# Two-bank context attention, early first weights of an eight-expert stage, and sixteen experts' weights kept in a 32-expert stage

## The chip, the cores and the metric

The kernel runs on one core of one Trainium2 chip. It is one launch that holds a whole four-layer decoder. The metric is the device time of one execution in microseconds, less is better; the time before is the median of three runs.

## The reference

The input x has 8 sequences of 256 tokens with 256 features; a context of 120 tokens with 192 features belongs to each sequence. Twelve sublayers follow each other, each as x = layernorm(x + f(x)). All is float32. The three that the change touches are these:

```
# L0 ffn: 8 experts, the best one for each token
e = argmax(softmax(x @ gate_w));  out = p[e] * (gelu(x @ w1[e] + b1[e]) @ w2[e] + b2[e])
# L1 ffn: 32 experts, the best four, at most 256 tokens for each, and one shared expert
probs, idx = top_k(softmax(x @ gate_w.T), 4);  weights = probs / sum(probs)
out = sum_k weights[k] * ((silu(g) * u) @ w_down[idx[k]]),  g, u = split(x @ w_gate_up[idx[k]])
out += (silu(gs) * us) @ shared_w_down
# L3 xattn: 8 heads of 64, keys and values from the context
out = softmax(q @ k.T * 64**-0.5) @ v,  then out @ Wo + bo
```

## The kernel before, in words

Activations are kept transposed in SBUF as xT, 128 partitions by 2 halves by 2048 tokens. The stages run one after the other. Each is made of blocks; in a block every engine has its own instruction list, engines are ordered by semaphores alone (`wait_ge`, `then_inc`), and a block begins when all engines have ended the one before. Each stage ends with a layer norm. SP issues plain DMAs, POOL (GpSimd) the indirect ones, each in program order; nothing is planned automatically.

**L3x, the context attention of layer 3** (`attention_stage`, the branch from L688). There are 16 units u, a sequence and half of the heads each. For a unit TensorE computes the scores (L725) into banks 0 and 1, VectorE takes their maxima (L828), TensorE turns these (L735) into bank 7, ScalarE copies them negated (L792), TensorE computes the turned scores less the maxima (L748, L753) into banks 2 and 3, ScalarE takes the exponential (L809) into PT, and TensorE forms the value products in bank 4 (L765) and the sums of the exponentials in bank 6 (L768). ScalarE inverts the sums as exp(-ln(sum)) (L799 and L801); VectorE (`divide`) corrects this inverse by one Newton step in two instructions (L837, L838) and multiplies the value products by it (L839). TensorE's order in the loop is: turned scores of u, values of u-1, maxima of u+1, scores of u+2. The values of a unit wait for its exponential and for `at_done` of the unit before (L761), as bank 4 and bank 6 are used by every unit. VectorE's order is maxima of u, then division of u-2.

**L0f, the eight-expert stage** (`moe_top1_stage`). The first block routes: TensorE and VectorE compute each token's expert and its slot in the array slots_x in HBM (`slot`) and, for each tile of 256 slots, which expert's weights it needs (`weight_row`, then `routed`). POOL then scatters the rows of each of 16 token tiles into slots_x (L1455); ahead of each scatter but the first it waits until all before have landed (L1454, semaphore `put`). Behind the scatters it issues two indirect gathers of the weights of tiles 0 and 1 (L1424, 2.1 MB each) and waits for `put`. In the same block TensorE and VectorE go on with the bias term and the sum (L1495, L1561). The second block works through 15 tiles: SP loads the slots (L1589), TensorE transposes (L1627), multiplies up (L1639) and down (L1652); POOL gathers weights two tiles ahead.

**L1f, the 32-expert stage** (`moe_top4_stage`). Block one routes on TensorE and VectorE (L2467 to L2532) while SP prefetches only the next stage's packed weights. Block two: TensorE transposes x, ScalarE copies it into rows (L2591), POOL scatters each tile four times into picks_x (L2549, 64 scatters), and the shared expert is computed beside that. Block three loops over 32 experts. SP loads for expert e its weights into `we` (L2634, four slots) and its picked rows into `xe` (L2635, four slots), both counted on one semaphore; the loads for e+4 are issued when ScalarE has finished expert e (`y_done`). TensorE's order is transposes of e+2 (L2667), up of e+1 (L2677), down of e (L2687). ScalarE does the silu (L2706) and the scaled copy out (L2714), VectorE the copy of the transposes (L2729), the product (L2754) and the places of the results (`place`). POOL scatters the results in two DMAs per expert into picks_y (L2652), and ScalarE writes ye of e+2 only when those of e have landed. A fourth block reads picks_y back and sums.

Of the kernel before, what the change touches and what calls it, by code (L numbers as in the profile page):

```python
# [18 lines left out]
P = 128  # L19
# [34 lines left out]
def columns(*fields):  # L54
    at, out = 0, {}
    for name, n in fields:
# [46 lines left out]
           "y_ready", "mean_ready", "d_ready", "sq_ready", "var_ready", "x_ready", "veps_ready", "ln_ready",  # L103
# [5 lines left out]
           "got_head2", "got_head3", "zeroed", "filled", "ticked", "routed", "centred", "used", "dotted", "placed", "blanked", "sent_even", "sent_odd", *(f"tile{t}" for t in range(16)),  # L109
# [143 lines left out]
def attention_stage(nc, c, name):  # L253
# [55 lines left out]
    with ExitStack() as ctx:  # L309
# [378 lines left out]
        else:  # L688
# [3 lines left out]
            with ExitStack() as part:  # L692
# [4 lines left out]
                cor = sb("cor", [P, 2 * SEQ], F32, part)  # L697
# [10 lines left out]
                with nc.Block() as block:  # L708
# [5 lines left out]
                    def _(pe):  # L714
# [103 lines left out]
                    def _(dve):  # L818
# [12 lines left out]
                        def divide(u):  # L831

                            b, half = units[u]
                            guess = inv[:, u % 2, :]
# [562 lines left out]
def moe_top1_stage(nc, c, ins):  # L1397
# [16 lines left out]
    with ExitStack() as ctx:  # L1414
# [14 lines left out]
        with ExitStack() as part:  # L1429
# [10 lines left out]
            with nc.Block() as block:  # L1440
# [5 lines left out]
                def _(pool):  # L1446

                    pool.wait_ge(s["filled"].sem, FILLS[0] * 16)
                    pool.wait_ge(s["routed"].sem, s["routed"].at(1))
                    for t in range(NT):  # L1450
                        pool.wait_ge(s["row_ready"].sem, s["row_ready"].at(t + 1))
                        if t:

                            pool.wait_ge(s["put"].sem, s["put"].at(16 * t))  # L1454
# [3 lines left out]
                    gather_weights(0)  # L1458
# [967 lines left out]
def moe_top4_stage(nc, c, ins):  # L2426
# [9 lines left out]
    SLOTS = E * CAP  # L2436
    with ExitStack() as ctx:
# [5 lines left out]


        with ExitStack() as part:
# [168 lines left out]
        with ExitStack() as part:  # L2614
            NB = 4
            we = sb("we", [P, NB, 2 * 2 * I + D], F32, part)
# [11 lines left out]
            with nc.Block() as block:  # L2628
                @block.sync
                def _(sp):  # L2630
                    def load(e):

                        k = e % NB
                        sp.dma_start(we[:, k, :], ins["L1f_w"][e]).then_inc(s[x_in[k]].sem, 16)  # L2634
                        sp.dma_start(xe[:, k, :, :], c.picks_x[e * CAP:(e + 1) * CAP, :]  # L2635
                                     .rearrange("(q p) d -> p q d", p=P)).then_inc(s[x_in[k]].sem, 16)
                    for e in range(NB):
                        load(e)
                    for e in range(E):
# [19 lines left out]
                def _(pe):  # L2659
                    def turn(e):  # L2660

                        pe.wait_ge(s[x_in[e % NB]].sem, s[x_in[e % NB]].at(32 * (e // NB + 1)))
# [8 lines left out]
                    def up(e):  # L2671
                        pe.wait_ge(s["evac_a"].sem, s["evac_a"].at(e + 1))
                        if e >= 2:
                            pe.wait_ge(s["hidden"].sem, s["hidden"].at(e - 1))
                        for g in range(2):
                            for j in range(DH):
                                mm = nc.tensor.matmul(ps[:, 2 + e % 2, g * CAP:(g + 1) * CAP],  # L2677
                                                      we[:, e % NB, j * 2 * I + g * I:j * 2 * I + g * I + I],
# [3 lines left out]
                    def down(e):  # L2682
# [3 lines left out]
                        for q in range(2):  # L2686
                            mm = nc.tensor.matmul(ps[:, 4 + e % 2, q * D:(q + 1) * D], a[:, e % 2, q * P:(q + 1) * P],  # L2687
                                                  we[:, e % NB, 4 * I:4 * I + D], start=True, stop=True)
                        mm.then_inc(s["down_pe"].sem, 1)
                    turn(0)  # L2690
# [33 lines left out]
                def _(dve):  # L2724
# [8 lines left out]
                    def place(e):  # L2733

                        k = e % NB
                        dve.wait_ge(s[x_in[k]].sem, s[x_in[k]].at(32 * (e // NB + 1)))
# [688 lines left out]
```

## Time and profile before

| | us |
|---|---|
| median of 3 runs | 3403.5 (3394.33 to 3407.84) |
| profiled execution | 3397.96 |
| its span, first to last instruction | 3396.1 |
| TensorE matmuls busy | 2415.3 |
| VectorE busy | 1693.9 |
| ScalarE busy | 937.2 |
| GpSimd busy | 787.2 |

Busy times overlap, and their sum says nothing of the span. The mean granted TensorE clock is 0.855 of full speed; the clock has two levels in this trace. Line numbers (L765) are those of the kernel. Times in a timeline are microseconds from the span's start: L0f lies from about 335 on, L1f from 1190, L3x's attention loop from 3056 to 3167. An entry in brackets is the idle time of the engine ahead of the instruction and what ended it.

### The profile page before, as it was taken

Reading aid. Unit: us, or ns where it says so; the run is one execution under the profiler, and the core shown is the slowest. Engines: PE = TensorE matmul, PEld = TensorE weight load, DVE = VectorE, ACT = ScalarE, POOL = GpSimd, SP = SyncE. Lnnn points to the kernel's source line nnn. Section 1 sums busy time; section 2 is a strip of 40 time slices with the busy share of each in tenths; the row PEclk is TensorE's granted clock in tenths of the full one; section 3 lists DMA queues with packets and bytes.
Section 4 is the critical chain, followed back from the end, with each engine's and each line's share of the span. In section 5 each row is a group of like instructions: output and inputs, shape, how many; then the busy total and the mean of one; then the engine's idle time right before and its main releaser. Section 6 shows DMA issues by size and latency. Waiting matters only on the chain. (4 is left out here: it accounts for less than half of the span.)

```text
span 3396.1 us, 38901 instructions
## 1 busy us (share of the span) xinstructions
PE 2415.3 (71%) x13893; PEld 1562.2 (46%) x13899; DVE 1693.9 (50%) x4532; ACT 937.2 (28%) x1761; POOL 787.2 (23%) x772
## 2 busy tenths in 40 slices
PE   6777489798776652758763565777777776488786
PEld 4534278645434332633441222666666654236332
DVE  4644100148446631353746567556656636534387
ACT  0232022110430410221141232433333323223244
POOL 1000200230010034411000001777777760100000
PEclk9889599899997966977996578899899887799898
DMA  6200145334015114635001002422222210000000
GB/s 168 65 14 17 63 147 186 121 93 126 20 42 143 26 62 143 221 145 99 4 23 62 0 0 83 103 54 58 54 56 57 63 38 25 0 25 1 0 0 25
DMA packets 125964, 223.41 MB, mean 66 GB/s; under 512 B 38550, under 2 KB 76182, under 8 KB 122208
## 3 DMA queue, kind: packets, MB, share of 16 engines
q1 hardware_dynamic: 72688, 116.33, 12.1%
q0 software_dynamic: 51952, 100.65, 9.7%
q10 hardware_dynamic: 1152, 4.19, 0.3%
q8 instruction: 101, 1.65, 0.2%
q14 instruction: 71, 0.58, 0.1%
HBM read 240.93 MB, written 62.59 MB: 89 GB/s over the span
## 5 line engine op out<-in xcount | busy, mean ns | idle before, releaser
L2897 POOL DMA_INDIRECT L2f_G<-in_L2f_table,L2f_idx x512 | 523.1, 1022 | 232.0 <-issue 155.8
L2954 PE MATMUL psum<-L2f_G,L2f_diag 128*128 128x256 f32 x1024 | 299.8, 458 | 172.7 <-ACT L2f_diag L3024 172.7
L2954 PEld LDWEIGHTS psum<-L2f_G,L2f_diag 128*128 128x128 f32 x1024 | 232.9, 233 | 237.2 <-ACT L2f_diag L3024 196.0
L3132 DVE CUSTOM_DVE_ANT_0 L2f_junk<-L2f_G,L2f_X 128x256 bf16<-128x256 f32 x512 | 182.7, 421 | 257.0 <-DMA L2f_G<-in_L2f_table,L2f_idx 257.0
L3024 ACT ACTIVATE L2f_diag<-const,L2f_actd 128x128 f32<-128x128 f32 x528 | 161.2, 388 | 25.2 <-DVE L2f_actd L3146 25.0
L1156 PE MATMUL psum<-constb 128*128 128x256 bf16 x512 | 83.9, 290 | 82.0 <-ACT L2a_PT L1323 24.3
L2931 PE MATMUL psum<-xT,L2f_mw 128*128 128x256 f32 x512 | 122.5, 383 | 0.0
L2549 POOL DMA_INDIRECT picks_x<-L1f_rows,L1f_put x64 | 61.5, 960 | 246.1 <-ACT L1f_rows L2591 227.3
L1639 PE MATMUL psum<-L0f_xeT,L0f_we 128*128 128x256 f32 x480 | 108.7, 386 | 0.9 <-DVE L0f_xeT L1674 0.9
L1652 PE MATMUL psum<-L0f_we,L0f_h 128*128 128x256 f32 x480 | 106.1, 380 | 0.0
L1323 ACT ACTIVATE L1a_PT<-psum 128x1536 f32<-128x1536 f32 x32 | 46.4, 1450 | 207.3 <-PE psum L1291 207.3
L2931 PEld LDWEIGHTS psum<-xT,L2f_mw 128*128 128x128 f32 x512 | 97.3, 193 | 12.9 <-issue 0.2
L1156 PEld LDWEIGHTS psum<-constb 128*128 128x128 bf16 x512 | 41.8, 101 | 129.5 <-ACT L1a_PT L1323 32.9
L3017 ACT ACTIVATE L2f_actd<-L2f_dots 128x9 f32<-128x9 f32 (+1 forms) x64 | 13.5, 211 | 317.2 <-DVE L2f_dots L3132 317.2
L991 PE MATMUL psum<-xT,weights 128*128 128x512 f32 x192 | 89.5, 630 | 16.0 <-PEq L236 11.0
L1639 PEld LDWEIGHTS psum<-L0f_xeT,L0f_we 128*128 128x128 f32 x480 | 93.2, 194 | 14.1 <-issue 1.3
L1652 PEld LDWEIGHTS psum<-L0f_we,L0f_h 128*128 128x128 f32 x480 | 90.3, 191 | 11.4
L1666 ACT ACTIVATE L0f_h<-psum,L0f_we 128x256 f32<-128x256 f32 x120 | 50.3, 470 | 155.3 <-PE psum L1639 155.3
L2652 POOL DMA_INDIRECT picks_y<-L1f_ye,L1f_home x64 | 61.3, 958 | 93.7 <-ACT L1f_ye L2714 83.0
L2196 POOL PARTITION_ALL_REDUCE L2x_gm<-L2x_mx x4 | 1.4, 357 | 349.2 <-issue 325.8
L2667 PE MATMUL psum<-const,L1f_xe 128*128 128x128 f32 x128 | 22.5, 303 | 82.9 <-DMA L1f_xe<-picks_x 82.5
L1674 DVE COPY L0f_xeT<-psum 128x512 f32<-128x512 f32 x15 | 10.4, 692 | 138.4 <-PE psum L1627 138.4
(670 smaller groups left out, 5162.9 us busy)
## 6 DMA issues: line engine op xcount, KB each, us to landing
L1f_we<-in_L1f_w SPq DMA_DIRECT2D x32, 384.0 KB, 3.1
picks_x<-zeros SPq DMA_DIRECT2D x16, 544.0 KB, 8.9
L1f_xe<-picks_x SPq DMA_DIRECT2D x32, 272.0 KB, 3.7
picks_y<-zeros SPq DMA_DIRECT2D x16, 512.0 KB, 7.0
L2f_G<-in_L2f_table,L2f_idx POOLq DMA_INDIRECT x512, 2.8
slots_x<-zeros POOLq DMA_DIRECT2D x8, 512.0 KB, 7.5
L1f_g<-picks_y SPq DMA_DIRECT2D x8, 512.0 KB, 10.9
L1f_g<-picks_y ACTq DMA_DIRECT2D x8, 512.0 KB, 12.0
```

The lines of the kernel that those rows point to most:

```text
L991: mm = nc.tensor.matmul(dst, wt[rows, j * m + g * P:j * m + g * P + P], source[rows, j, bass.ds(col, n)], start=(k == 0), stop=(k == len(t ...
L1156: nc.tensor.matmul(out, c.one, m.broadcast_to([P, 2, P]), start=True, stop=False, skip_group_check=True)
L1639: mm = nc.tensor.matmul(ps[:, f // 2, (f % 2) * TILE:(f % 2 + 1) * TILE], we[:, k, j * F + f * P:j * F + f * P + P], xeT[:, k, j, :], star ...
L1652: mm = nc.tensor.matmul(ps[:, 6 + k, q * D:(q + 1) * D], h[:, k, f, q * P:(q + 1) * P], we[:, k, W2 + f * D:W2 + (f + 1) * D], start=(f == ...
L1666: nc.scalar.activation(h[:, k, f, :], ps[:, f // 2, (f % 2) * TILE:(f % 2 + 1) * TILE], ACT.Gelu, bias=we[:, k, B1 + f:B1 + f + 1]).then_i ...
L2549: nc.gpsimd.indirect_dma_start(out=c.picks_x[:, :], out_offset=bass.IndirectOffsetOnAxis(ap=put[:, t, k:k + 1], axis=0), in_=rows[:, t, :] ...
L2652: nc.gpsimd.indirect_dma_start(out=c.picks_y[:, :], out_offset=bass.IndirectOffsetOnAxis(ap=home[:, e % NB, q:q + 1], axis=0), in_=ye[:, e ...
L2897: nc.gpsimd.indirect_dma_start(out=G[:, h, k, :], out_offset=None, in_=ins["L2f_table"], in_offset=bass.IndirectOffsetOnAxis(ap=IDX[:, t, ...
L2931: mm = nc.tensor.matmul(ps[:, UP_BANK + i % 2, chunk(g)], wt[:, j * F + f * P:j * F + f * P + P], c.xT[:, j, chunk(k)], start=(j == 0), st ...
L2954: mm = nc.tensor.matmul(ps[:, MIX_BANK + t % 2, 0:D], diag[:, i % 2, k, :], row[:, D:2 * D], start=(h == 0 and k == 0), stop=(h == HEADS - ...
L3024: e = nc.scalar.activation(diag[:, i % 2, k, :], c.ident, ACT.Copy, scale=act_d[:, i % 2, k:k + 1])
L3132: e = V.tensor_tensor_reduce(out=junk[:, k, :], in0=row[:, 0:D], in1=X[:, t % 3, :], scale=1.0, scalar=0.0, op0=ALU.mult, op1=ALU.add, acc ...
```

## The change

In L3x the value products go to bank 4 or 5 in turn. They wait for the logarithm of the unit before (which has read bank 6) and for the division of the unit before that. The Newton step is left out: the division is one multiplication by exp(-ln(sum)). In L0f the gather of the first tile's weights is issued ahead of the scatters, and a scatter no longer waits for the ones before. In L1f a buffer of 16 experts' weights lives from the routing to the end of the expert loop. SP issues the first 16 loads in the routing block; TensorE waits for all of them at the head of the expert loop. In the loop SP loads only xe for e+4 when expert e is done and, behind it, the weights of e+16 into the slot that e has left. The semaphore counts follow.

```diff
@@ L3x, TensorE values(u)
-                                pe.wait_ge(s["at_done"].sem, s["at_done"].at(u))
+                                pe.wait_ge(s["ln_ready"].sem, s["ln_ready"].at(u))
+                            if u >= 2:
+                                pe.wait_ge(s["at_done"].sem, s["at_done"].at(u - 1))
-                                nc.tensor.matmul(ps[rows_of(i), 4, j * SEQ:(j + 1) * SEQ], V[0:CTX, b, h * hd:(h + 1) * hd],
+                                nc.tensor.matmul(ps[rows_of(i), 4 + u % 2, j * SEQ:(j + 1) * SEQ], V[0:CTX, b, h * hd:(h + 1) * hd],
@@ L3x, VectorE divide(u)
-                            link(nc.vector.tensor_tensor(cor[:, :], ps[:, 6, :], guess, ALU.mult))
-                            link(nc.vector.scalar_tensor_tensor(cor[:, :], cor[:, :], -2.0, guess, ALU.add, ALU.mult))
-                            nc.vector.scalar_tensor_tensor(AT[:, 2 * half:2 * half + 2, b * SEQ:(b + 1) * SEQ],
-                                                           ps[:, 4, :].rearrange("p (g q) -> p g q", g=2), -1.0,
-                                                           cor[:, :].rearrange("p (g q) -> p g q", g=2), ALU.mult, ALU.mult)\
+                            nc.vector.tensor_tensor(AT[:, 2 * half:2 * half + 2, b * SEQ:(b + 1) * SEQ],
+                                                    ps[:, 4 + u % 2, :].rearrange("p (g q) -> p g q", g=2),
+                                                    inv[:, u % 2, :].rearrange("p (g q) -> p g q", g=2), ALU.mult)\
                                 .then_inc(s["at_done"].sem, 1)
@@ L0f, POOL in the routing block
+                    gather_weights(0)
                     for t in range(NT):
                         pool.wait_ge(s["row_ready"].sem, s["row_ready"].at(t + 1))
-                        if t:
-                            pool.wait_ge(s["put"].sem, s["put"].at(16 * t))
                         nc.gpsimd.indirect_dma_start(
...
-                    gather_weights(0)
                     gather_weights(1)
@@ L1f, SP in the routing block
                     c.prefetch(sp, name)
+                    for e in range(NW):
+                        sp.dma_start(we[:, e, :], ins["L1f_w"][e]).then_inc(s["w_first"].sem, 16)
@@ L1f, SP in the expert loop
-                        sp.dma_start(we[:, k, :], ins["L1f_w"][e]).then_inc(s[x_in[k]].sem, 16)
                         sp.dma_start(xe[:, k, :, :], c.picks_x[e * CAP:(e + 1) * CAP, :]
                                      .rearrange("(q p) d -> p q d", p=P)).then_inc(s[x_in[k]].sem, 16)
+                    def load_weights(e):
+                        if e >= NW + 2:
+                            sp.wait_ge(s[w_in[e % 2]].sem, s[w_in[e % 2]].at(16 * ((e - NW) // 2)))
+                        sp.dma_start(we[:, e % NW, :], ins["L1f_w"][e]).then_inc(s[w_in[e % 2]].sem, 16)
...
                         if e + NB < E:
                             load(e + NB)
+                        if e + NW < E:
+                            load_weights(e + NW)
@@ L1f, TensorE
                     def up(e):
                         pe.wait_ge(s["evac_a"].sem, s["evac_a"].at(e + 1))
+                        if e >= NW:
+                            pe.wait_ge(s[w_in[e % 2]].sem, s[w_in[e % 2]].at(16 * ((e - NW) // 2 + 1)))
...
+                    pe.wait_ge(s["w_first"].sem, s["w_first"].at(16 * NW))
                     turn(0)
```

NW is 16 (experts' weights held), NB is 4 (slots of xe), CAP is 256.

## Rows read from the trace of the kernel before

**Rows 1.** The page's first part: busy us, share of the span, instructions of each engine.
```profile
PE 2415.3 (71%) x13893; PEld 1562.2 (46%) x13899; DVE 1693.9 (50%) x4532; ACT 937.2 (28%) x1761; POOL 787.2 (23%) x772
```

**Rows 2.** Timeline, one L3x unit: start us, us, engine, line, what, idle before.
```profile
3096.80 0.69 DVE L837 TENSOR_TENSOR L3x_cor<-psum,L3x_inv 128x512 f32<-128x512 f32 x1 [3.00 <-ACT L3x_inv L801]
...
3097.42 0.60 PE L753 MATMUL psum<-L3x_MT,const 64*120 64x256 f32 x4
...
3098.26 0.69 DVE L839 SCALAR_TENSOR_TENSOR L3x_AT<-psum,L3x_cor 128x512 f32<-128x512 f32 x1
...
3099.09 1.08 PE L765 MATMUL psum<-L3x_PT,L3x_V 120*64 120x256 f32 x8 [1.08 <-ACT L3x_PT L809]
...
3101.72 0.59 ACT L799 ACTIVATE L3x_inv<-psum 128x512 f32<-128x512 f32 x1
...
3102.33 0.60 PE L748 MATMUL psum<-L3x_Q,L3x_K 64*120 64x256 f32 x4
...
3105.30 1.09 PE L765 MATMUL psum<-L3x_PT,L3x_V 120*64 120x256 f32 x8 [1.07 <-ACT L3x_PT L809]
```

**Rows 3.** Waits, 3055 to 3170: total us, times, longest.
```profile
PE psum L765 <- ACT L3x_PT L809: 14.0, 13, 1.1
...
PE psum L765 <- DVE L3x_AT L839: 5.0, 2, 3.6
```

**Rows 4.** Timeline, last L3x unit.
```profile
3160.60 1.98 PE L765 MATMUL psum<-L3x_PT,L3x_V 120*64 120x256 f32 x8 [3.61 <-DVE L3x_AT L839]
```

**Rows 5.** Timeline, L0f from the first scatter to the first tile load.
```profile
365.64 1.08 POOL L1455 DMA_INDIRECT slots_x<-L0f_rows,L0f_slot  x1 [73.86 <-DVE L0f_weight_row L1552]
...
390.23 1.22 DVE L1561 TENSOR_TENSOR L0f_acc<-psum,xT 128x1024 f32<-128x1024 f32 x1 [3.87 <-PE psum L1495]
...
413.75 0.96 POOL L1455 DMA_INDIRECT slots_x<-L0f_rows,L0f_slot  x1 [2.22 <-DMA slots_x<-L0f_rows,L0f_slot]
...
416.31 0.96 POOL L1424 DMA_INDIRECT L0f_we<-in_L0f_w,L0f_weight_row  x1 [0.30 <-DMA slots_x<-L0f_rows,L0f_slot]
429.80 4.45 SPq L1589 DMA_DIRECT2D L0f_xe<-slots_x  x3
```

**Rows 6.** The tile L0f_we: landing of the 15 weight gathers.
```profile
DMA to landing us min/median/max: 8.8/9.2/12.5
```

**Rows 7.** Timeline, L1f: last scatter, first loads, first up projection.
```profile
1314.04 0.96 POOL L2549 DMA_INDIRECT picks_x<-L1f_rows,L1f_put  x1 [0.30 <-issue]
1322.16 0.36 SPq L2634 DMA_DIRECT2D L1f_we<-in_L1f_w  x1
...
1330.16 3.62 PE L2677 MATMUL psum<-L1f_xeT,L1f_we 128*128 128x256 f32 x8
```

**Rows 8.** Timeline, L1f expert loop: first and last reload, and two experts between.
```profile
1337.89 0.33 SPq L2634 DMA_DIRECT2D L1f_we<-in_L1f_w  x1
...
1354.33 0.33 SPq L2634 DMA_DIRECT2D L1f_we<-in_L1f_w  x1
...
1354.70 0.44 SPq L2635 DMA_DIRECT2D L1f_xe<-picks_x  x1
...
1358.86 0.66 PE L2667 MATMUL psum<-const,L1f_xe 128*128 128x128 f32 x4 [1.49 <-DMA L1f_xe<-picks_x]
...
1363.01 0.33 SPq L2634 DMA_DIRECT2D L1f_we<-in_L1f_w  x1
...
1453.74 0.33 SPq L2634 DMA_DIRECT2D L1f_we<-in_L1f_w  x1
```

**Rows 9.** DMA issues of L1f and L0f: KB each, median us to landing.
```profile
L1f_xe<-picks_x SPq DMA_DIRECT2D x32, 272.0 KB, 3.7
...
L0f_xe<-slots_x SPq DMA_DIRECT2D x3, 256.0 KB, 2.7
```

**Rows 10.** Windows: length, busy by engine, PE clock, DMA share, GB/s; routing, return loads.
```profile
1190.00:1232.00 42.00, 14.43 (x65) 13.79 (x66) 24.43 (x100) 0.63 (x1) 0.00 (x0) 0.50 0.07 26
...
1477.00:1505.00 28.00, 11.03 (x32) 4.62 (x32) 22.07 (x48) 0.00 (x0) 0.00 (x0) 0.50 0.76 301
```

More of the change, by code:

```diff
@@ L102 @@
            "negmax", "probs", "turned", "evac_a", "evac_b", "mixed", "normed", "at_ready", "at_evac", "out_ready",
-           "y_ready", "mean_ready", "d_ready", "sq_ready", "var_ready", "x_ready", "veps_ready", "ln_ready",
+           "y_ready", "mean_ready", "d_ready", "sq_ready", "var_ready", "x_ready", "ln_ready",
            "root_ready", "exp_ready", "newton", "dve_chain", "loaded", "pack_even_landed", "pack_odd_landed", "route_pe", "route_dve",
@@ L108 @@
            "x_even", "x_odd", "y_even", "y_odd", "y_done", "got_even", "got_odd", "got_head0", "got_head1",
-           "got_head2", "got_head3", "zeroed", "filled", "ticked", "routed", "centred", "used", "dotted", "placed", "blanked", "sent_even", "sent_odd", *(f"tile{t}" for t in range(16)),
+           "got_head2", "got_head3", "zeroed", "filled", "ticked", "routed", "used", "placed", "blanked", "sent_even", "sent_odd", "w_first", "w_even", "w_odd", *(f"tile{t}" for t in range(16)),
            *(f"expert{k}" for k in range(4)),
@@ L696, in attention_stage @@
                 inv = sb("inv", [P, 2, 2 * SEQ], F32, part)
-                cor = sb("cor", [P, 2 * SEQ], F32, part)
                 ones = sb("ones", [P, P], F32, part)
@@ L2436, in moe_top4_stage @@
     SLOTS = E * CAP
+    NB, NW = 4, 16
+    WE = 2 * 2 * I + D
+    w_in = ("w_even", "w_odd")
     with ExitStack() as ctx:
@@ L2442, in moe_top4_stage @@
         acc = sb("acc", [P, DH, T])
+        early = ctx.enter_context(ExitStack())
+        we = sb("we", [P, NW, WE], F32, early)
         with ExitStack() as part:
@@ L2614, in moe_top4_stage @@
         with ExitStack() as part:
-            NB = 4
-            we = sb("we", [P, NB, 2 * 2 * I + D], F32, part)
             xe = sb("xe", [P, NB, 2, ROW], F32, part)
@@ L2660, in turn @@
                     def turn(e):
-                        pe.wait_ge(s[x_in[e % NB]].sem, s[x_in[e % NB]].at(32 * (e // NB + 1)))
+                        pe.wait_ge(s[x_in[e % NB]].sem, s[x_in[e % NB]].at(16 * (e // NB + 1)))
                         if e >= 2:
@@ L2677, in up @@
                                 mm = nc.tensor.matmul(ps[:, 2 + e % 2, g * CAP:(g + 1) * CAP],
-                                                      we[:, e % NB, j * 2 * I + g * I:j * 2 * I + g * I + I],
+                                                      we[:, e % NW, j * 2 * I + g * I:j * 2 * I + g * I + I],
                                                       xeT[:, e % 2, j, :], start=(j == 0), stop=(j == DH - 1))
@@ L2687, in down @@
                             mm = nc.tensor.matmul(ps[:, 4 + e % 2, q * D:(q + 1) * D], a[:, e % 2, q * P:(q + 1) * P],
-                                                  we[:, e % NB, 4 * I:4 * I + D], start=True, stop=True)
+                                                  we[:, e % NW, 4 * I:4 * I + D], start=True, stop=True)
                         mm.then_inc(s["down_pe"].sem, 1)
+                    pe.wait_ge(s["w_first"].sem, s["w_first"].at(16 * NW))
                     turn(0)
@@ L2735, in place @@
                         k = e % NB
-                        dve.wait_ge(s[x_in[k]].sem, s[x_in[k]].at(32 * (e // NB + 1)))
+                        dve.wait_ge(s[x_in[k]].sem, s[x_in[k]].at(16 * (e // NB + 1)))
                         if e >= NB:
@@ L2761, in moe_top4_stage @@
             for k, n in dict(turned=E, evac_a=E, hidden_pe=E, hidden=E, down_pe=E, gated=E, y_done=E,
-                             expert0=16 * E // 2, expert1=16 * E // 2, expert2=16 * E // 2, expert3=16 * E // 2, sent_even=16 * E, sent_odd=16 * E, placed=E).items():
+                             expert0=4 * E, expert1=4 * E, expert2=4 * E, expert3=4 * E,
+                             w_first=16 * NW, w_even=8 * (E - NW), w_odd=8 * (E - NW), sent_even=16 * E, sent_odd=16 * E, placed=E).items():
                 s[k].base += n
+        early.close()
         with ExitStack() as part:
```

1 line of the change is left out of this document (removed).

## The prediction

> **What bounds the kernel now.** I read the page's busy shares first: TensorE has 71% of the span [rows 1], so no engine is a wall, and the twelve stages have limits of their own. I therefore read each of the three stages that the diff touches by its timeline, and then its waits and DMA landings. In the attention loop of the last context stage (L3x) one unit takes 6.21 us. The reader is to see in it that TensorE ends the turned scores at 3098.02, stands still for 1.08 us, and starts the value products only when VectorE's third instruction has freed the bank at 3098.95 [rows 2]. The trace names the exponential L809 as releaser, but the one that the products need was over a unit earlier, and the products' loads begin before this one ends. So I read the 13 such waits as waits for `at_done` [rows 3]. In the eight-expert stage (L0f) the routing ends with 16 scatters that run one by one, 3.2 us apart, while the last VectorE work is over at 391.45; the tile loop's first load is issued at 429.80 [rows 5]. In the 32-expert stage (L1f) TensorE waits in the expert loop for the picked rows (xe), not for weights: two experts take 8.68 us from issue to issue, of which 4.16 lie between the issue of xe and the first transpose [rows 8].
>
> **Attention, two banks and one division.** Removed: two VectorE instructions of 0.69 us in each of 16 units. Moved: the value products of unit u now need the division of u-2 and the logarithm of u-1 instead of the division of u-1. Added wait: the logarithm (`ln_ready`). Everything later on TensorE queues behind it. It ends at 3102.31 [rows 2], one unit ahead of the products at 3105.3, which could start at the earliest at 3104.2, so it is hidden by 1.9 us. If this cover went, the unit would lengthen by what is missing. What is late next is TensorE itself: 6.21 - 1.08 = 5.13 us per unit. VectorE has less to do than before, ScalarE the same. The maxima copy keeps its distance, since it hangs on TensorE's own order. Sum: 13 units x 1.08 = 14.0. The two last ones waited 5.0 in total [rows 3]: of unit 14's 1.42 I take 1.1; unit 15 waited 3.61 [rows 4] and will wait for one logarithm only, about 0.8, so 2.8. The final division loses two instructions: 1.4. Unit 15's first eight products took 1.98 at the lower clock after that idle time, against 1.08 in a usual unit [rows 2, 4]; with both sets, 1.7. Together 21.0. Bounds: 15 (the logarithm's wait costs half of each stall again, or the clock still falls) and 25 (the output projection behind it also starts at the full clock).
>
> **Eight-expert stage.** The first gather of weights moves ahead of the scatters: 1.26 us in POOL's queue. Each scatter no longer waits until the one before has landed. The nearest row for a scatter behind a scatter is L1f's: 0.96 busy and 0.30 idle, 1.26 us apart [rows 7]. From 365.64: gather, 16 scatters, second gather issued at 365.64 + 17 x 1.26 = 387.1 instead of 416.31, so 29.2 earlier. Beside them TensorE and VectorE do their bias products until 391.45 as before. What is late next is the second gather's landing, since 13.49 us pass from its issue to SP's next DMA [rows 5], far more than the block's change on other engines needs. Two gathers in flight land after up to 12.5, a single one in 9.2 [rows 6]. With the first long landed I take off half of the 3.3 us between these: gain 31. Bounds: 22 (the 2.1 MB of the first gather stand ahead of the scatters in the same queue and hold them for a whole 9.2 us), 34 (it ends with VectorE). If the scatters' speed needed VectorE's silence it would be lost here, since four adds now run beside them.
> [...]
>
> **32-expert stage.** Sixteen more DMAs on SP's queue during routing, behind the next pack's load: 16 x 0.36 us of issue [rows 7] = 6 us, and 6.3 MB, 21 us at the 301 GB/s of this stage's own return loads [rows 10]. Routing lasts 42 us and the DMA engines carried 26 GB/s in it [rows 10], so both are hidden, and the wait `w_first` at the head of TensorE's queue costs nothing. If the cover were gone (loads slower than 150 GB/s), all experts would start later. Below nothing I bound it by -3: something else that must come by DMA in these 42 us meets the loads and lands 1 us later, as xe does behind one of them [rows 9], three times. I take 0. The 64 scatters between routing and experts stay: POOL paces them.
> Start of the loop: before, four pairs of loads were issued from 1322.16 and the first up projection began at 1330.16 [rows 7]. Now only xe is loaded: 1322.16 + 2.7 to 3.7 for landing, then two sets of transposes, 0.66 each at the full clock [rows 8] and twice that at the low one, beside the second of which the first is copied: about 1328. Gain 2.2.
> In the loop: y_done(e), SP issues xe(e+4), landing, transpose, up, down, two copies, y_done(e+2). From 1358.86 to 1363.01 that tail is 4.15 [rows 8]; with 0.37 for the weights' issue ahead and 4.16 for xe it makes 8.68. The 0.37 goes for certain. xe lands in 3.7 with 384 KB ahead of it in the same queue; the nearest load without such a forerunner, 256 KB for L0f, lands in 2.7 [rows 9]. The return scatters stay, so I take 2.9. Per expert: (0.37 + 0.8) / 2 = 0.585; 28 loads, 16.4. Mean pace 4.29 (27 intervals from 1337.89 to 1453.74 [rows 8]) becomes 3.7. The weights for expert e+16 are issued behind xe(e+4), so that they delay only a load that comes 3.7 us later; TensorE waits for them sixteen experts later, which costs nothing, and SP's new waits for earlier weight loads neither. What is late next: the same chain, then TensorE's own work of some 3 us per expert, and the return scatters. Bounds: 0.37/2 x 28 = 5, and (0.37 + 1.0)/2 x 28 = 19 plus some low-clock stretches saved. Sum for the stage 19.
>
> **The sum.** 21 + 31 + 19 = 71. The profiled execution took 3397.96 (span 3396.10, 1.86 around it); less 71 is 3327. It stood 5.5 below the median of the three runs (3403.5) and 3 below the mean of all four, 3401. I forecast from this mean: 3330.
>
> **Rivals.**
> (a) The picked rows land no sooner: the early weights are off the path. For it: what TensorE waits for is xe, never weights [rows 8], and 272 KB in 256 short rows may need its 3.7 by itself. Against: L0f's 2.7 [rows 9]. Then only SP's 0.37 counts, 5 instead of 16.4: 3341. The same figure holds if the return scatters take over at 3.9 per expert. Chance 0.22.
> (b) The L0f scatters don't overlap, because the gather blocks them or each is served alone: pace 3.2 stays. L1f's 64 scatters speak against it. The stage then gains 2 (one gather in flight at the end): 3359. Chance 0.05.
> (c) The clock holds. Where TensorE stands still for 3.61 us, its next products run at the 1.2 GHz level [rows 4]. With shorter waits in both loops and a shorter gap ahead of the output projection, stretches at 1.2 GHz go too. A burst there costs nearly its own length again (1.98 against 1.08 [rows 2, 4]); 9 us of it less in three places: 3321. The Trainium skill has this as a rule: "TensorE: Matmul & The Clock Gate", section "HAM oscillation", idle gaps between bursts throttle the clock anew. Chance 0.12.
> (d) Slower. Both loops get denser on TensorE, and the granted clock falls to 1.2 GHz for their length. L3x: 16 units x 5.1 = +82; L1f: 28 experts x 3.0 = +84; 3496. It decides once the low level holds for more than two fifths of both loops. Against: units at 83% busy run at the full level now [rows 2]. Chance 0.03, with all else that could lose 71 us.
> My own case, all three paid as worked out, has 0.58: 3330, between 3319 and 3343.
>
> **How the numbers follow.** About 0.5% (17 us) is what a measurement of this kernel can tell from no change. (a) and (c) lie within 3312 to 3352, which also takes in the lower ends of two terms at once, not of all three (22 + 15 + 5: 3359). Faster by over 0.5%: 0.96; within: 0.01; slower: 0.03.
>
> **What would show it.** L3x: units 5.1 us apart, no idle time ahead of the value products but in the last, one VectorE instruction of 0.69 per division. L0f: POOL's DMAs 1.26 us apart, SP's first tile load 29 to 34 us sooner after routing. L1f: sixteen 384 KB loads over before routing ends, xe landing in 2.9, the loop's issues 3.7 apart. The prediction is wrong if the scatters stay 3 us apart, if xe still needs 3.7, or if TensorE waits for the logarithm.

## The result, and the profile after

| | before | after |
|---|---|---|
| median, us | 3401.3 (4 runs) | 3325.1 (4 runs, 3316.55 to 3328.6) |
| profiled execution | 3397.96 | 3316.55 |
| its span | 3396.1 | 3314.7 |

The ratio is 0.9775, 95% interval 0.9754 to 0.9796: the changed kernel is 76 us faster (69 to 84), where 3330 was forecast, 71 us. Its profiled execution is the shortest of its four, so the terms are compared by stage. The page's first part, beside [rows 1]:

```profile
PE 2402.9 (72%) x13893; PEld 1553.9 (47%) x13899; DVE 1672.6 (50%) x4500; ACT 937.5 (28%) x1761; POOL 787.6 (24%) x772
```

VectorE has 32 instructions less, two for each of 16 units. Its busy time fell by 21.3 us, that of TensorE's matmuls by 12.4, the others' by less. So most of the time saved is time in which TensorE had stood still.

**L3x.** Timeline of one unit, which answers to [rows 2], and of the last one:

```profile
3029.19 0.69 DVE L836 TENSOR_TENSOR L3x_AT<-psum,L3x_inv 128x512 f32<-128x512 f32 x1 [3.30 <-ACT L3x_inv L802]
...
3030.33 1.08 PE L766 MATMUL psum<-L3x_PT,L3x_V 120*64 120x256 f32 x8
...
3035.39 0.87 PE L766 MATMUL psum<-L3x_PT,L3x_V 120*64 120x256 f32 x6
...
3083.36 1.08 PE L766 MATMUL psum<-L3x_PT,L3x_V 120*64 120x256 f32 x8 [0.74 <-issue]
...
3086.63 0.69 DVE L836 TENSOR_TENSOR L3x_AT<-psum,L3x_inv 128x512 f32<-128x512 f32 x1 [1.99 <-ACT L3x_inv L802]
...
3087.65 9.66 PE L863 MATMUL psum<-L3x_AT,weights 128*128 128x512 f32 x18 [2.34 <-PEq L707]
```

The products start 5.06 us apart (3030.33 and 3035.39) with no bracket, so without idle time. One division of 0.69 us is left. The last products wait 0.74 us instead of 3.61 and run at the full clock, 1.08 against 1.98 [rows 4]. The output projection of the kernel before:

```profile
3167.78 12.66 PE L866 MATMUL psum<-L3x_AT,weights 128*128 128x512 f32 x22 [3.80 <-PEq L708]
```

From the first scores to the output projection the stage takes 89.6 us (2998.08 to 3087.65) instead of 111.7 (3056.05 to 3167.78): 22.2 less. The output projection's first result reaches VectorE 8.84 us after its start instead of 10.13: 1.3 more.

**L0f.** The last routing instruction before, and behind it the timeline after, from that instruction to the first tile load, which answers to [rows 5]:

```profile
364.58 0.17 DVE L1552 CAST L0f_weight_row<-L0f_owner 128x15 uint32<-128x15 f32 x1
```

```profile
360.68 0.17 DVE L1546 CAST L0f_weight_row<-L0f_owner 128x15 uint32<-128x15 f32 x1
...
361.76 1.09 POOL L1421 DMA_INDIRECT L0f_we<-in_L0f_w,L0f_weight_row  x1 [74.22 <-DVE L0f_weight_row L1546]
...
369.62 0.97 POOL L1450 DMA_INDIRECT slots_x<-L0f_rows,L0f_slot  x1 [0.30 <-issue]
369.73 1.22 DVE L1555 TENSOR_TENSOR L0f_acc<-psum,xT 128x1024 f32<-128x1024 f32 x1 [8.08 <-PE psum L1489]
370.89 0.97 POOL L1450 DMA_INDIRECT slots_x<-L0f_rows,L0f_slot  x1 [0.30 <-issue]
...
383.63 0.98 POOL L1421 DMA_INDIRECT L0f_we<-in_L0f_w,L0f_weight_row  x1 [0.30 <-issue]
385.01 1.23 DVE L1555 TENSOR_TENSOR L0f_acc<-psum,xT 128x1024 f32<-128x1024 f32 x1 [3.87 <-PE psum L1489]
393.47 4.50 SPq L1583 DMA_DIRECT2D L0f_xe<-slots_x  x3
```

POOL's DMAs stand 1.27 us apart, also the one that began while VectorE was in its first add. From the last routing instruction (it starts at 360.68, before at 364.58) to the first tile load it is 32.8 us instead of 65.2: 32.4 less. The block now ends long after VectorE (386.24); 9.84 us pass from the second gather's issue to SP's load, 13.49 before. The scatters are issued at their own pace, but the first eight land later than before, 2.6 to 7.8 us after their issue beside the first gather's 2.1 MB, where a scatter alone took 2.4.

**L1f.** Timeline: the early loads in the routing, the head of the loop, two experts, and the first load that reads the results back:

```profile
1153.35 8.34 SPq L2460 DMA_DIRECT2D L1f_we<-in_L1f_w  x16
...
1285.27 1.92 SPq L2632 DMA_DIRECT2D L1f_xe<-picks_x  x4
...
1290.03 2.50 PE L2683 MATMUL psum<-L1f_xeT,L1f_we 128*128 128x256 f32 x5
...
1300.72 0.36 SPq L2632 DMA_DIRECT2D L1f_xe<-picks_x  x1
...
1301.13 0.51 SPq L2638 DMA_DIRECT2D L1f_we<-in_L1f_w  x1
...
1304.61 0.36 SPq L2632 DMA_DIRECT2D L1f_xe<-picks_x  x1
1304.79 0.66 PE L2671 MATMUL psum<-const,L1f_xe 128*128 128x128 f32 x4 [1.08 <-DMA L1f_xe<-picks_x]
...
1418.78 1.28 SPq L2781 DMA_DIRECT2D L1f_g<-picks_y  x3
```

The same load before:

```profile
1477.14 2.87 SPq L2772 DMA_DIRECT2D L1f_g<-picks_y  x4
```

The DMA issues of the loop, median landing last, beside [rows 9]:

```profile
L1f_xe<-picks_x SPq DMA_DIRECT2D x32, 272.0 KB, 2.9
...
picks_y<-L1f_ye,L1f_home POOLq DMA_INDIRECT x64, 2.6
```

Windows of the routing and of two parts of the loop (columns as in [rows 10]):

```profile
1153.00:1195.00 42.00, 14.44 (x65) 13.81 (x66) 24.44 (x100) 0.63 (x1) 0.00 (x0) 0.50 0.45 175
1304.00:1344.00 40.00, 33.85 (x171) 27.84 (x172) 18.47 (x65) 12.80 (x32) 19.97 (x21) 1.00 0.77 244
1357.00:1397.00 40.00, 35.26 (x180) 29.15 (x179) 19.27 (x69) 13.44 (x33) 21.10 (x22) 1.00 0.47 150
```

The early loads put 175 GB/s on the routing's idle DMA engines, and from the next pack's load to the loop's first it takes 132.3 us, before 132.2: they cost nothing. The first up projection begins 4.76 us behind the first load instead of 8.00 [rows 7]. The picked rows land in 2.9 us instead of 3.7. From the first load of the loop to the first one that reads the results back it takes 133.5 us (1285.27 to 1418.78) instead of 155.0 (1322.16 to 1477.14): 21.5 less. The pace is 3.73 us per expert between 1304.61 and 1353.06, where weights are still loaded, and 3.63 afterwards (11 intervals from 1356.56 to 1396.49).

Not all of the 21.5 us is the queue's. In the loop before, TensorE fell twice to the lower clock level, and the changed loop has no such stretch:

```profile
1405.34 0.82 PE L2667 MATMUL psum<-const,L1f_xe 128*128 128x128 f32 x4 [2.05 <-DMA L1f_xe<-picks_x]
1405.95 3.46 PE L2677 MATMUL psum<-L1f_xeT,L1f_we 128*128 128x256 f32 x8
...
1439.99 1.11 PE L2667 MATMUL psum<-const,L1f_xe 128*128 128x128 f32 x4 [2.28 <-DMA L1f_xe<-picks_x]
1440.89 3.05 PE L2677 MATMUL psum<-L1f_xeT,L1f_we 128*128 128x256 f32 x8
```

Transposes and up projection of one expert take 4.28 and 4.16 us there, and 2.55 (0.66 + 1.89) at the full level: 3.3 us in all. All seven traces with this loop as it was (before, e1 to e6) have such stretches; between 4 and 21 of the 256 up-projection matmuls are slow in them, beside those of the loop's head. The traces of the changed kernel, of its repeat e9 and of e7 have none. The seven loops last 152.6 to 157.1 us, so a few us between two traces of L1f can be the execution's own.

22.2 + 32.4 + 21.5 + 1.3 = 77 us. These two executions differ by 81.4; the other 4 lie ahead of L0f, in stages that the change leaves alone (the last routing instruction starts at 360.68 instead of 364.58). The medians differ by 76.

### The profile page after: what moved, and what is told of

It reads as the page before. It is cut to its first block and busy times, and to the rows that moved or that the text cites. A ratio compares the mean times of both kernels' runs of the same rounds, so it can differ in the third digit from the quotient of the medians.

```text
span 3314.7 us, 38855 instructions
## 1 busy us (share of the span) xinstructions
PE 2402.9 (72%) x13893; PEld 1553.9 (47%) x13899; DVE 1672.6 (50%) x4500; ACT 937.5 (28%) x1761; POOL 787.6 (24%) x772
## 3 DMA queue, kind: packets, MB, share of 16 engines
q1 hardware_dynamic: 72688, 116.33, 12.4%
## 5 line engine op out<-in xcount | busy, mean ns | idle before, releaser
L1788 PE MATMUL psum<-L3f_h,weights 128*128 128x512 f32 x128 | 62.1, 630 | 22.1 <-DVE L3f_h L1859 22.0
L1421 POOL DMA_INDIRECT L0f_we<-in_L0f_w,L0f_weight_row x15 | 14.2, 948 | 264.9 <-PE psum L1646 190.4
## 6 DMA issues: line engine op xcount, KB each, us to landing
L1f_g<-picks_y SPq DMA_DIRECT2D x8, 512.0 KB, 12.3
L1f_g<-picks_y ACTq DMA_DIRECT2D x8, 512.0 KB, 12.3
```

The lines of the kernel that those rows point to most:

```text
L1788: mm = nc.tensor.matmul(ps[:, 4 + 2 * (n % 2) + o, :], w["w2"][:, f * D + o * P:f * D + o * P + P], h[:, u % 2, i * CH:(i + 1) * CH], star ...
```

## The experiments

The stages run one after the other, so each experiment is read by its stage in the trace, and by the ratio of the whole where that is wide enough. The first four ran on a chip on which the kernel before takes 3514.7 us (the untouched stage L2f alone takes 838.6 instead of 736.1 us there), the others on chips where it takes 3398 to 3399; ratios are always within one chip.

### e1, attention part alone


> The kernel before with the attention part of the change alone (two banks and one division). Theory: the three parts lie in stages that run one after the other and add up, so this one gives what the changed kernel's L3x shows: units 5.06 us apart, L3x shorter by 22 us, ratio 0.9935. Rival: part of the 22 us belongs to the run and not to the change, or to the other two parts (a shifted clock): then L3x is shorter by under 18 us.


Measured: ratio 0.9919 (0.9881 to 0.9958); units 5.06 us apart; first scores to output projection 3156.4 to 3246.0, 89.6 us as in the changed kernel. On the same chip e4, which leaves this stage alone, has 111.8. The 22 us belong to this part, and it does not lean on the others.

### e2, one division, one bank
```diff
-                            link(nc.vector.tensor_tensor(cor[:, :], ps[:, 6, :], guess, ALU.mult))
-                            link(nc.vector.scalar_tensor_tensor(cor[:, :], cor[:, :], -2.0, guess, ...))
+                            nc.vector.tensor_tensor(AT[...], ps[:, 4, :]..., inv[:, u % 2, :]..., ALU.mult)
                             # values(u) still waits for at_done.at(u), still bank 4
```


> The kernel before with the Newton step left out, but the value products still in one bank and still behind the division of the unit before. Theory: what binds before is one cycle, sums end, logarithm, exponential, three VectorE instructions, value products of the next unit, 6.21 us long. Without two instructions of 0.69 it is 4.83, under TensorE's own 5.06, so the second bank buys nothing: units 5.06 apart, no wait ahead of the value products but in the last units, L3x shorter by 20 to 22 us. Rival: the second bank is what frees TensorE: the wait for the division stays, and the unit falls by half of the stall or less, L3x shorter by under 12 us.


Measured: ratio 0.9947 (0.9918 to 0.9975). Its timeline, one unit:

```profile
3210.48 0.69 DVE L834 TENSOR_TENSOR L3x_AT<-psum,L3x_inv 128x512 f32<-128x512 f32 x1 [3.30 <-ACT L3x_inv L800]
...
3211.62 1.08 PE L764 MATMUL psum<-L3x_PT,L3x_V 120*64 120x256 f32 x8
...
3216.68 1.08 PE L764 MATMUL psum<-L3x_PT,L3x_V 120*64 120x256 f32 x8
```

The division ends at 3211.17, 0.45 us before TensorE is ready for the products at 3211.62, and the unit takes 5.06 us with one bank. The stage takes 92.5 us (3164.2 to 3256.7), 19.2 less than before, a little under the 20 to 22 of the first theory. Its mechanism holds: inside the loop the second bank buys nothing. The 2.9 us that two banks add lie at the end, where no other work stands ahead of the last products: they wait 2.2 us for the division there (0.74 in the changed kernel), and they and the sums behind them then run partly at the lower clock level, 1.73 and 1.98 us against 1.08 and 1.06. What the Newton step was there for is a better inverse; no run here measures what leaving it out costs in accuracy.

### e3, two banks, Newton step kept
```diff
-                            if u:
-                                pe.wait_ge(s["at_done"].sem, s["at_done"].at(u))
+                            if u >= 2:
+                                pe.wait_ge(s["at_done"].sem, s["at_done"].at(u - 1))
                             ...  # products into bank 4 + u % 2
+                            if u:
+                                pe.wait_ge(s["at_done"].sem, s["at_done"].at(u))
                             ...  # sums of the exponentials, bank 6
```


> The kernel before with the value products in bank 4 or 5 in turn, but the Newton step kept: since it reads bank 6, only the sums of the exponentials still wait for the division of the unit before. Theory (one cycle through the division): only the four value products, half of 1.08, move out of the cycle, 6.21 becomes 5.67, L3x shorter by 13 x 0.54 = 7 us, at most 9. Rival (the second bank is what frees TensorE): units 5.1 apart, L3x shorter by 14 us or more.


Measured: ratio 0.9962 (0.994 to 0.9984); the stage 96.6 us (3187.0 to 3283.6), 15.1 less. Its timeline, one unit:

```profile
3219.96 1.08 PE L765 MATMUL psum<-L3x_PT,L3x_V 120*64 120x256 f32 x8
...
3220.27 0.69 DVE L841 SCALAR_TENSOR_TENSOR L3x_AT<-psum,L3x_cor 128x512 f32<-128x512 f32 x1
...
3221.01 0.63 PEld L770 LDWEIGHTS psum<-L3x_PT,L3x_ones 120*64 120x64 f32 x8 [0.42 <-DVE L3x_AT L841]
...
3225.26 1.08 PE L765 MATMUL psum<-L3x_PT,L3x_V 120*64 120x256 f32 x8
```

The size in my expectation was wrong: 1.08 us are the value products alone, the sums take as much again, so 1.08 and not 0.54 moved out of the cycle. The 15.1 us are what the rival had forecast (14 or more), and the whole time alone would speak for it; what speaks against it is the trace. The cycle is still there: the sums wait 0.42 us for the division and the unit takes 5.31 us, where the rival had 5.1 and no wait. Either edit alone brings most of the 22 us; the division is the better half (19.2), and it needs no bank.

### e4, eight-expert part alone


> The kernel before with the eight-expert part alone (first gather ahead of the scatters, no wait between scatters). Theory: parts add up; from the last routing instruction to the first tile load 33 us instead of 65, ratio 0.9905. Rival: the gain of the stage hangs on what lies before it in the changed kernel (the run's own 3.8 us ahead of this stage): 28 us or less here.


Measured: ratio 0.9914 (0.9886 to 0.9942), 32.7 us from the last routing instruction to the first tile load (364.7 to 397.5), as in the changed kernel. So this part and that of L3x each bring alone what they bring in the changed kernel. The L1f part was not run alone as it stands.

### e5, no waits between the scatters, both gathers behind them


> The eight-expert part with the scatters' waits gone, but both gathers of weights behind the scatters as before. Theory: the waits were the cost (16 x 1.9 us), the place of the first gather is worth little: second gather issued at the same time as in the changed kernel (17 DMAs 1.27 us apart), but two gathers in flight at the end, so the first tile load comes 2 to 4 us later than in the changed kernel; the stage gains 29 us. Rival: with the 2.1 MB of the first gather no longer ahead of them the scatters land sooner and the block ends sooner: gain 33 or more.


Measured: ratio 0.9903 (0.9874 to 0.9932); 357.3 to 393.4, 36.1 us, 29.1 less than before. Its timeline:

```profile
378.75 1.00 POOL L1424 DMA_INDIRECT L0f_we<-in_L0f_w,L0f_weight_row  x1 [0.30 <-issue]
380.05 0.96 POOL L1424 DMA_INDIRECT L0f_we<-in_L0f_w,L0f_weight_row  x1 [0.30 <-DMA slots_x<-L0f_rows,L0f_slot]
...
393.41 0.89 SPq L1586 DMA_DIRECT2D L0f_xe<-slots_x  x2
```

13.36 us from the second gather to SP's load, as before (13.49); with the first gather long landed it is 9.84. So the waits are worth 29 us and the early first gather 3.3.

### e6, both gathers ahead of the scatters
```diff
                     gather_weights(0)
+                    gather_weights(1)
                     for t in range(NT):
                         ...
-                    gather_weights(1)
```


> The eight-expert part with both gathers ahead of the scatters. Theory: in the changed kernel the block ends with the landing of the second gather, 9.8 us behind its issue, since no other engine works then. With both ahead it ends with VectorE's last sum or the last scatter's landing: first tile load 6 to 7 us sooner than in the changed kernel, the stage gains 38 to 39 us. Rival: what ends the block is POOL's drain of its queue or the scatters' landing behind 4.2 MB: the first tile load comes at most 2 us sooner, gain 34 or less.


Measured: ratio 0.9868 (0.9838 to 0.9898); 362.5 to 389.8, 27.3 us, 37.9 less than before. Its timeline:

```profile
385.43 0.97 POOL L1454 DMA_INDIRECT slots_x<-L0f_rows,L0f_slot  x1 [0.30 <-issue]
388.12 1.22 DVE L1558 TENSOR_TENSOR L0f_acc<-psum,xT 128x1024 f32<-128x1024 f32 x1 [3.87 <-PE psum L1492]
389.79 0.89 SPq L1586 DMA_DIRECT2D L0f_xe<-slots_x  x2
```

SP's load follows VectorE's last add (which ends at 389.34) by 0.45 us. So what ended the block in the changed kernel was the second gather in flight: POOL waits there for nothing but the scatters, and still the next block did not begin until the gather had landed. The landings say the same: the second gather landed 12.5 us behind its issue before, 12.3 in e5, 8.8 in the changed kernel, and SP's load came 1.0 to 1.1 us behind the landing in all three. This is 5.5 us better than the changed kernel (6 to 7 were expected), and VectorE is now the end.

### e7, rows ahead of the weights, nothing else
```diff
-                        sp.dma_start(we[:, k, :], ins["L1f_w"][e]).then_inc(s[x_in[k]].sem, 16)
                         sp.dma_start(xe[:, k, :, :], ...).then_inc(s[x_in[k]].sem, 16)
+                        sp.dma_start(we[:, k, :], ins["L1f_w"][e]).then_inc(s[w_in[k]].sem, 16)
@@ up(e)
+                        pe.wait_ge(s[w_in[e % NB]].sem, s[w_in[e % NB]].at(16 * (e // NB + 1)))
```


> The kernel before with one edit in the 32-expert loop: for each expert SP issues the picked rows ahead of its weights, each on a semaphore of its own; transposes wait for the rows alone, the up projection for the weights. No early weights, no 16 slots. Theory A (what the change bought is that the rows no longer stand behind 384 KB; that the weights come early is not needed): loop 12 to 17 us shorter, issues 3.7 to 3.9 apart. Theory B (the traffic of 384 KB per expert itself slows the rows, wherever it stands in the queue, and the weights now arrive late for the up projection): loop at most 6 us shorter, TensorE waits for the weights. In the changed kernel the rows land in 3.0 us (3.6 at those with weights beside them) where weights are still loaded and in 2.7 where they are not, which speaks for A in the larger part.


Measured: ratio 0.9958 (0.9943 to 0.9973); loop 136.9 us (1324.7 to 1461.6), 18.1 less than before, of the changed kernel's 21.5. Its timeline:

```profile
1344.32 0.36 SPq L2635 DMA_DIRECT2D L1f_xe<-picks_x  x1
1344.53 0.66 PE L2668 MATMUL psum<-const,L1f_xe 128*128 128x128 f32 x4 [1.11 <-DMA L1f_xe<-picks_x]
1344.73 0.47 SPq L2637 DMA_DIRECT2D L1f_we<-in_L1f_w  x1
1345.02 1.89 PE L2679 MATMUL psum<-L1f_xeT,L1f_we 128*128 128x256 f32 x8
```

The up projection stands right behind the transposes, without a bracket: the weights, though loaded only four experts ahead and behind the rows, are there. The rows land in 3.0 us. Theory A holds, though 18.1 is more than its 12 to 17: this loop has none of the low-clock stretches, which are worth 3.3 us in the trace of the kernel before. 16 experts' weights in SBUF and their load during routing account for 3.4 us (1.4 against the repeat e9), which is within the 4.5 us by which unchanged loops differ. What can be placed of it is an up projection 0.9 us earlier at the head of the loop (5.7 us behind the first load here, 4.8 there), and an end, in which no weights are loaded, that is 1.4 us shorter (from the last load of rows to the first that reads back: 23.7 us here, 22.3 there).

### e8, eight slots for the picked rows
```diff
-    NB, NW = 4, 16
+    NB, NW = 8, 16
```


> The kernel before with the 32-expert part of the change, and eight slots for the picked rows instead of four (rows of expert e+8 are loaded when e is done). Theory: the loop is still bound by the chain from the end of expert e over the load of the rows of e+4 to its transposes, 3.7 us per expert while weights are loaded and 3.35 afterwards. With eight slots this chain leaves the path; next is TensorE's own work of some 3.0 us or the return scatters (1.27 x 2 and landing, every second expert's buffer): pace 3.0 to 3.2, loop shorter than in the changed kernel (133.5 us) by 8 to 16 us, though eight loads at the start cost up to 1 us. Rival: the second chain, the results' buffer behind its scatters' landing, has the same length as the first: pace stays at 3.4 or more and the loop is at most 5 us shorter.


L3x and L0f are as in the kernel before. Measured: ratio 0.9937 (0.9912 to 0.9961); loop 125.1 us (1325.3 to 1450.4), 8.4 less than in the changed kernel, at the lower end of what the theory said. Waits of the loop (total us, times, longest):

```profile
ACT L1f_ye L2727 <- DMA picks_y<-L1f_ye,L1f_home: 55.3, 25, 6.9
...
PE psum L2677 <- DMA L1f_xe<-picks_x: 52.9, 1, 52.9
```

TensorE's transposes no longer wait for rows but once, ahead of the loop. In their place ScalarE waits for the return scatters, 25 times where it was once before (1.9 us). A timeline of this kernel shows how:

```profile
1387.60 0.85 ACT L2727 ACTIVATE L1f_ye<-psum,L1f_own 128x256 f32<-128x256 f32 x2
...
1389.47 0.96 POOL L2662 DMA_INDIRECT picks_y<-L1f_ye,L1f_home  x1 [0.30 <-issue]
...
1395.67 0.84 ACT L2727 ACTIVATE L1f_ye<-psum,L1f_own 128x256 f32<-128x256 f32 x2 [6.94 <-DMA picks_y<-L1f_ye,L1f_home]
```

Two experts' results come out together (1386.61 and 1387.60) and their four scatters are issued 1.27 us apart. The results of the second next expert need the same buffer and wait until its two scatters have landed. Here, in the longest such wait, the second of them was issued at 1389.47 and took 6.1 us, beside two loads of rows and two of weights; the next results start at 1395.67, 9.1 us behind those of 1386.61. The other pairs from 1371 on are 6.1 to 7.7 us apart. The mean is 3.3 us per expert, which is neither the 3.0 to 3.2 of the theory nor the 3.4 or more of the rival: stretches at TensorE's pace (38.19 busy of 40 us from 1345 on) come first, such pairs afterwards. A short stretch at the lower clock level (7 slow up-projection matmuls about 1400) is also in it.

The ratio stands for 21 us, by its interval 13 to 30, where the stage gained 30. Stages that this kernel leaves alone took 9 us more in its profiled execution, whose mean granted clock is 0.850 against 0.855 before; the cause of that is open.

### e9 and e10, the changed kernel again, and with both additions
e10 is the changed kernel with the edits of e6 and e8.


> The changed kernel as it is, on the same chip as the next two. Theory: ratio 0.977 to 0.979 and the three stages as before: 33 us to the first tile load in L0f, loop of 133.5 us in L1f, units of 5.06 us in L3x. If the 76 us were partly the run's own, the ratio here would lie outside 0.975 to 0.980.

> The changed kernel with two more edits: both weight gathers of the eight-expert stage ahead of the scatters, and eight slots for the picked rows in the 32-expert loop. Theory: both gains found alone add up, 5.5 us (first tile load 27.3 us behind the routing instead of 32.8) and 8.4 us (loop 125.1 instead of 133.5): 14 us less than the changed kernel, ratio to it 0.996, to the kernel before 0.973. Rival: the unchanged stages give it back (with eight slots alone the whole execution was only 20 us shorter where its stage was 30 us shorter): under 5 us less than the changed kernel.


Measured in five executions of each on one chip: e9 3320.3 us, ratio 0.9766 (0.9749 to 0.9783); e10 3309.0 us, ratio 0.9744 (0.9725 to 0.9762). By stage e9 has 33.1 us, 135.5 us and 88.2 us (L0f, L1f loop, L3x), which is 75 us less than before. e10 has 27.3 us and 129.4 us in the first two: 5.7 and 6.1 less than e9, together 12, and the medians are 11.3 apart, where 14 were expected. The intervals overlap, so the whole does not prove it by itself; the 27.3 us of L0f are the same in e6 and e10. The loop gains 8.4 us in e8 and 6.1 here; ScalarE waits 63.7 us for scatters here, and 12 up-projection matmuls behind the loop's head run at the lower clock level, 7 in e8. e10 has the lowest median of all versions. Four buffers of results, which would be the next step in L1f, were not tried: the scatters of different experts into one array would then be unordered.

### e11, eight row slots, four weight slots, weights ahead of rows in the loop
```diff
                         sp.wait_ge(s["y_done"].sem, s["y_done"].at(e + 1))
                         if e + NB < E:
+                            load_weights(e + NB)
+                        if e + NX < E:
+                            load(e + NX)
```


> The kernel before with swapped order (rows and weights on semaphores of their own) and eight slots for the picked rows, but still four slots of weights, each loaded when its expert is done, ahead of the rows of e+8. No early weights. Theory: only the place of the rows matters; the weights of e+4 are wanted by an up projection three experts later (about 7 us of chain over 3 experts) and stay hidden: loop 126 to 129 us, as with 16 experts' weights (125.1), so the big buffer is worth 1 to 4 us. Rival: 656 KB per expert in 3.3 us, some 200 GB/s, delays the return scatters and the rows: 131 us or more.


Measured: ratio 0.9966 (0.9956 to 0.9977); loop 142.8 us (1321.1 to 1464.0). Missed: only 12.1 less than before, and 6 us more than e7 with four slots. Landings and waits of its loop:

```profile
L1f_xe<-picks_x SPq DMA_DIRECT2D x32, 272.0 KB, 4.8
...
picks_y<-L1f_ye,L1f_home POOLq DMA_INDIRECT x64, 3.9
```
```profile
ACT L1f_ye L2724 <- DMA picks_y<-L1f_ye,L1f_home: 71.0, 20, 6.7
```

Rows and scatters land later than in any other version, and ScalarE waits 71.0 us for scatters. The rival names the cause, traffic, but its condition (200 GB/s in the loop) is also met by the kernel before (220 GB/s), whose return scatters land in 3.3 us. Against e7 the run changes two things: in the loop the rows stand behind the weights again, as in the kernel before (the cut above shows it; only for the first four experts do the rows go first), and there are eight slots for them. Against e8 it keeps the weights' loads in the loop for all experts. The first up projection also begins 7.5 us behind the first load. So it does not say which of these costs the time, and it does not test its own theory: e7's order with eight slots was not run. What it does show is that eight slots with weights ahead of rows are slower than four slots with rows ahead (142.8 against 136.9 us).

## Why the prediction was right

**L3x, 21.0 forecast, 22.2 measured.** The reading of [rows 2, 3] was the step that carried it: the wait which the trace put down to the exponential L809 was one for the division of the unit before. e2 shows that directly, since nothing but VectorE's two instructions changed there and the wait went. Next came TensorE, as forecast (5.13, measured 5.06). The 0.07 per unit over 13 units is most of the difference. What I did not see is that one of the two edits would have done inside the loop: by [rows 2] the products are 1.08 us late and the Newton step takes 1.38 us, which is enough.

**L0f, 31 forecast, 32.4 measured.** The second gather's issue moved from 51.7 us behind the last routing instruction to 22.9: 28.8, forecast 29.2. The landing term was mis-sized: I took half of the 3.3 us between one gather and two in flight, and it is the whole, 3.65 (13.49 to 9.84). e5 confirms it from the other side. VectorE's adds cost the scatters nothing: the one in flight at 369.73, when the first add began, was followed 1.27 us later by the next, like all others. Three of the four adds ran beside the scatters; the last began at 385.01, behind the second gather. That the second gather's landing would end the block was forecast, and the landings listed at e6 bear it out; that it could be moved away too, for another 5.5 us, I did not see.

**L1f, 19 forecast, 21.5 measured.** Start 3.2 (forecast 2.2). Loop 18.3 (forecast 16.4): landing 2.9 and 3.7 us per expert are as worked out, but the way there is partly luck. The mean pace of 4.29 that I started from contains the two low-clock stretches, 3.3 us, which my sum held at nothing. The 27 intervals between reloads gained 17.1 us; without these stretches it is 13.8, where the shorter chain alone was to bring 15.8 (27 x 0.585). So the chain was over-sized by 2 us, and the clock and a shorter end of the loop (1.1 us) made up for it. e7 shows that the term was put in the right place: what is saved is the 0.37 of issue and 0.8 of landing that the rows lost to the weights ahead of them, not the time of the weights.

**Rivals.** (a) is refuted by the landing of 2.9; (b) by scatters 1.27 us apart; (d) by a granted clock of 1.00 from 1304 to 1397 and from 3025 on in L3x's units. (c) came true in part: L1f's loop lost its low stretches, 3.3 us, and the output projection is 1.3 us shorter, together some 5 us and not 9; that the last products run at 1.08 was in my own sum. The output projection still starts at the low level (its first 18 in 9.66 us). That differs between executions: in e9 its longest matmul takes 0.667 us and not 1.061, and its first result reaches VectorE after 7.1 us, not 8.8. The stages together gained 77 us where the sum had 71; 4.6 of these 6 us are this clock, which the sum held at nothing.

## What to carry to other kernels

When a wait's named releaser has long been done, look for the cycle through the shared buffer and add up its members: shortening the cycle below the next engine's work is enough, and inside the loop a second buffer buys nothing more (here 2.9 us at its end). In a queue, put the load that is wanted now ahead of the load that is wanted four experts later, before spending memory on loading the latter early. Where a block ends with a transfer in flight that the next block wants only later, issue it ahead of the work that the end does depend on. And when a mean pace is the start of a sum, look first for stretches at the lower clock in it: they come off with another change than the one that is being priced.

## What the runs showed of the hardware

- Indirect scatters without a wait between them are issued 1.27 us apart, also behind gathers of 4.2 MB (e6); with a wait each took 3.2. They land later there, up to 7.8 us after issue behind one gather and 11.8 behind two, where 2.4 is usual, and the issue pace does not show it.
- The next block's first DMA comes 9.8 us behind a gather issued last (13.4 with two in flight), 1.0 us behind its landing, though no instruction waits for that gather; with none in flight it came 0.45 us behind the last instruction (e6).
- A 272 KB load lands in 3.7 us (median) behind 384 KB in the same queue, in 2.9 to 3.0 ahead of it, in 2.7 with no other load of SP beside it.
- TensorE's granted level fell in the L1f loop before where its longest waits were 2.05 and 2.28 us; at 1342.03 a wait of 2.02 us was followed by an up projection at the full level. In the changed loop, whose longest wait is 1.08 us, it did not fall. In L3x a wait of 1.08 us in every unit never lowered it, and one of 3.61 did.
- Faster loads do not spread evenly: once rows are no longer late (e8), experts' results pair up behind four scatters, and ScalarE stands still for up to 6.9 us at a time.
